# Turning the normalised inputs of a transformer block with transposing DMAs instead of TensorE

## The reference

```
x = x + layernorm(attention(layernorm(x)))
x = x + layernorm(ffn(layernorm(x)))

attention:  q, k, v = split(h @ w_qkv.T + b_qkv)         # h is the normalised input
            per chunk, with a state S (32 x 32) per head:
              out = (q * decay_q) @ S + ((q @ k.T) * mask) @ v
              S   = lam_c * S + (k * decay_k).T @ v
            out @ w_out.T + b_out
ffn:        gate = silu((h @ fp8(gate_w)) * gate_scale)  # fp8() rounds to e4m3, I = 1536
            up   = (h @ fp8(up_w)) * up_scale
            ((gate * up) @ fp8(down_w)) * down_scale
```

## Time and profile before

| | |
|---|---|
| median of three runs | 1149.89 us |
| profiled execution: span from first to last instruction | 1146.1 us |
| what lies around the span (1149.89 - 1146.1) | 3.8 us |
| busy: TensorE, DVE, POOL, ACT | 92%, 64%, 55%, 34% |
| one steady slot | 62.9 us |
| stack copies: number, size, time to landing | 480, 64 KB, 2.1 us |

### The profile page before, as it was taken

How to read it: one execution, slowest core, us unless ns; L and a number is a source line. 1 busy time by engine, 2 the same in 40 slices (tenths; PEclk the granted TensorE clock), 3 DMA queues, 4 the chain that set the end, 5 groups by cost and what they waited for, 6 DMA issues and landing times.

```text
span 1146.1 us, 23001 instructions
## 1 busy us (share of the span) xinstructions
PE 1053.1 (92%) x8772; PEld 795.6 (69%) x8772; DVE 738.0 (64%) x1415; ACT 391.7 (34%) x752; POOL 630.1 (55%) x659
## 2 busy tenths in 40 slices
PE   2646869999999999999999999999999999999887
PEld 1435549595968778595968677695959687786654
DVE  7869996574747475665747474666657475756542
ACT  3222435242433425152424334252424233342211
POOL 0557656474646565465647465555656464656433
PEclk9855979999999999999999999999999999999989
DMA  9211420403022120304031221204040312212000
GB/s 360 83 55 55 100 49 1 102 10 85 28 56 57 38 75 20 86 10 102 10 72 40 53 59 34 71 18 95 11 102 11 68 44 49 63 30 55 10 19 19
DMA packets 83629, 66.10 MB, mean 58 GB/s; under 512 B 9281, under 2 KB 70849, under 8 KB 83393
## 3 DMA queue, kind: packets, MB, share of 16 engines
q1 hardware_dynamic: 82656, 64.00, 21.6%
q10 hardware_dynamic: 864, 0.61, 0.2%
HBM read 24.72 MB, written 8.39 MB: 29 GB/s over the span
## 4 chain that ended last, share of the span: by engine, by line
PE 77%; DVE 13%; POOL 4%; issue 4%; DMA 1%; ACT 0%; POOLq 0%; DVEq 0%; SPq 0%
PE bank L513 29%; PE bank L621 13%; PE bank L528 11%; PE bank L603 6%; PE bank L635 5%; PE bank L565 3%; PE bank L569 2%; PE bank L552 2%; DVE stats L994 2%; PE bank L583 2%; POOL rstd L712 1%; PE bank L441 1%; DVE ffn_pool L932 1%; PE bank L595 1%; DVE up_q L939 1%
## 5 line engine op out<-in xcount | busy, mean ns | idle before, releaser
L788 POOL TENSOR_TENSOR att_pool<-p,att_pool 128x512 f16<-128x512 f32 x128 | 149.8, 1191 | 78.1 <-ACT att_pool L371 78.1
L513 PE MATMUL bank<-ffn_pool,gate_q 128*128 128x256 f16 x1536 | 185.1, 274 | 3.8 <-DVE ffn_pool L1209 3.8
L621 PE MATMUL bank<-x_hl,wqkv_hi 128*128 128x256 f16 x1024 | 172.2, 275 | 13.9 <-DVE wqkv_lo L923 13.9
L513 PE MATMUL bank<-ffn_pool,up_q 128*128 128x256 f16 x1536 | 184.2, 273 | 0.0
L528 PE MATMUL bank<-down_q,ffn_pool 128*128 128x512 f16 x768 | 170.7, 379 | 1.0 <-DVE ffn_pool L1099 1.0
L513 PEld LDWEIGHTS bank<-ffn_pool,gate_q 128*128 128x128 f16 x1536 | 148.9, 98 | 21.4 <-DVE ffn_pool L1209 4.1
L513 PEld LDWEIGHTS bank<-ffn_pool,up_q 128*128 128x128 f16 x1536 | 150.6, 98 | 18.1
L775 POOL TENSOR_TENSOR ffn_pool<-ffn_pool 128x512 f16<-128x512 f32 x96 | 111.2, 1158 | 94.4 <-ACT ffn_pool L385 92.9
L371 ACT CAST att_pool<-p 128x512 f16<-128x512 f32 x128 | 77.9, 618 | 190.7 <-DVE p L1089 190.7
L1099 DVE SCALAR_TENSOR_TENSOR ffn_pool<-bank,us_t,ffn_pool 128x256 f32<-128x256 f32 x192 | 84.1, 479 | 89.9 <-PE bank L513 87.7
L621 PE MATMUL bank<-x_hl,wqkv_lo 128*128 128x256 f16 x512 | 141.0, 275 | 0.0
(11 more groups left out here) (123 smaller groups left out, 1715.1 us busy)
## 6 DMA issues: line engine op xcount, KB each, us to landing
att_pool<-att_pool SPq DMA_DIRECT2D x480, 64.0 KB, 2.1
x_t<-in_x SPq DMA_DIRECT2D x16, 512.0 KB, 3.8
out_x<-ffn_pool SPq DMA_DIRECT2D x32, 256.0 KB, 2.1
att_pool<-in_w_qkv_t SPq DMA_DIRECT2D x4, 768.0 KB, 8.0
ffn_pool<-in_gate_w SPq DMA_DIRECT2D x4, 768.0 KB, 12.8
ffn_pool<-in_up_w SPq DMA_DIRECT2D x4, 768.0 KB, 4.2
ffn_pool<-in_down_w SPq DMA_DIRECT2D x4, 768.0 KB, 4.7
mask<-in_mask_c SPq DMA_DIRECT2D x1, 1024.0 KB, 16.9
```

The costliest lines, as they stand in the source:

```text
L513: ins = nc.tensor.matmul(b[:, j * TOK:(j + 1) * TOK], w[:, k, o * P:(o + 1) * P], x1_hl[:, part, k], start=(k == 0 and part == 0), stop=(k ...
L621: ins = nc.tensor.matmul(b_t[i % 2][:, j * TOK:(j + 1) * TOK], (wqkv_hi, wqkv_lo)[a][:, k, o * P:(o + 1) * P], x_hl[:, b, k], start=(k == ...
L788: nc.gpsimd.tensor_tensor(pr_hl[:, 1, heads(s, g)], by_head(p32[:, g % 2]), pr_hl[:, 0, heads(s, g)], ALU.subtract).then_inc(p_lo_d, 1)
```

## The change

The fp32 values in `nrm` are no longer turned by TensorE. ACT casts them to the hi half and DVE subtracts to the lo half while they are still tokens x channels, into a new tensor `nrm_hl` in SBUF; then SP turns both halves of a tile with one transposing DMA (128 partitions x 1024 fp16, 256 KB, as eight blocks of 128x128) straight into `x_hl` or `x1_hl`. There are four such DMAs in a slot, 64 in all. x1 is split at the end of slot s, behind each `x1_normalise`, and no longer at the start of slot s + 1. The waits of TensorE go to the new semaphores `x_turned` and `x1_turned`.

```diff
+        nrm_hl = sb("nrm_hl", [P, T, 2, D], F16)
@@ SP, start
                 for k in range(KT):
                     sp.dma_start(w_stage[:, k], w_qkv_t[k * P:(k + 1) * P, :]).then_inc(w_in[k], 16)
+                for t in range(T):
+                    turn_x(0, t)
                 for n in range(3):
                     sp.dma_start(stage_for(n), piece_in(n)).then_inc(f_in[n], 16)
...
                 for n in range(3, 12):
                     sp.wait_ge(f_q_d, n - 2)
                     sp.dma_start(stage_for(n), piece_in(n)).then_inc(f_in[n % 3], 16)
+                    if n == 8:
+                        for t in range(T):
+                            turn_x(1, t)
                 stack(1)
+                for t in range(T):
+                    turn_x1(0, t)
+
+            def turned(half, t):
+                return half[:, :, :, t * P:(t + 1) * P].rearrange("p s k c -> p (s k) c")
+
+            def turn_x(n, t):
+                sp.wait_ge(x_lo_d, 2 * n + t + 1)
+                sp.sem_inc(turn_seen, 1)
+                sp.dma_start_transpose(turned(x_hl, t), nrm_hl[:, t].rearrange("p s d -> p (s d)")
+                                       ).then_inc(x_turned, 16)
@@ SP, slot (turn_x1 is turn_x with x1_lo_d, x1_hl and x1_turned)
                 if nxt:
+                    for t in range(T):
+                        turn_x(s + 1, t)
                     stack(s + 1)
+                if att:
+                    turn_x1(s, 0)
+                if att and not nxt:
+                    turn_x1(s, 1)
                 store(s - 1, 0)
+                if att and nxt:
+                    turn_x1(s, 1)
@@ ACT
             def split_x(n):
-                for j in range(2):
-                    act.wait_ge(x_tr, 2 * n + j + 1)
-                    nc.scalar.copy(x_hl[:, 0, 2 * j:2 * j + 2].rearrange("p k t -> p (k t)"),
-                                   b_s[j][:, :]).then_inc(x_hi_d, 1)
+                if not (type(n) is int and n < 2):
+                    act.wait_ge(x1_turned, 32 * n - 32)
+                elif n == 1:
+                    act.wait_ge(x_turned, 32)
+                for t in range(T):
+                    act.wait_ge(nrm_d[LN_X], 2 * n + t + 1)
+                    nc.scalar.copy(nrm_hl[:, t, 0], nrm[:, t]).then_inc(x_hi_d, 1)
+
+            def split_x1(v, t):
+                act.wait_ge(x_turned, 32 * v + (64 if type(v) is not int or v < last else 32))
+                act.wait_ge(nrm_d[LN_X1], 2 * v + t + 1)
+                nc.scalar.copy(nrm_hl[:, t, 0], nrm[:, t]).then_inc(x1_hi_d, 1)
@@ ACT, end of slot
+                if att:
+                    split_x1(s, 0)
+                if nxt:
                     v_hi(s + 1)
+                if att:
+                    split_x1(s, 1)
@@ PE: transpose_x and the transposes at the slot's start are gone
             def gate_up(v, i):
                 if i == 0:
-                    pe.wait_ge(x1_lo_d, 2 * v + 2)
+                    if type(v) is int and v == 0:
+                        pe.wait_ge(norms_d, 3)
+                    else:
+                        pe.wait_ge(y2_d, 2 * v)
+                    pe.wait_ge(x1_turned, 32 * v + 32)
...
             def project_qk(n, i):
-                pe.wait_ge(x_lo_d, 2 * n + 2)
+                pe.wait_ge(x_turned, 32 * n + 32)
@@ DVE (x_lo likewise; the two subtractions from PSUM at the slot's start are gone)
+            def x1_lo(v, t):
+                dve.wait_ge(x1_hi_d, 2 * v + t + 1)
+                nc.vector.tensor_tensor(nrm_hl[:, t, 1], nrm[:, t], nrm_hl[:, t, 0], ALU.subtract
+                                        ).then_inc(x1_lo_d, 1)
@@ DVE, end of slot
                     x1_moments(s, m, 1)
                     v_sum(s + 1, 1)
                     x1_normalise(s, m, 1)
+                    x1_lo(s, 1)
                 y2_scale(v, 1)
```

More of the change, by code:

```diff
@@ L393, in slot @@
                 v = s - 1
-                for j in range(2):
-                    act.wait_ge(x1_tr, 2 * v + j + 1)
-                    nc.scalar.copy(x1_hl[:, 0, 2 * j:2 * j + 2].rearrange("p k t -> p (k t)"),
-                                   (b_y, b_att)[j][:, :]).then_inc(x1_hi_d, 1)
                 if att:
@@ L434, in _ @@
         def _(pe):
-            def transpose_x(n):
-                pe.wait_ge(nrm_d[LN_X], 2 * n + 2)
-                for j in range(2):
-                    for kk in range(2):
-                        for t in range(T):
-                            ins = nc.tensor.transpose(b_s[j][:, kk * TOK + t * P:kk * TOK + (t + 1) * P],
-                                                      nrm[:, t, (2 * j + kk) * P:(2 * j + kk + 1) * P], eye[:, :])
-                    ins.then_inc(x_tr, 1)
             def start():
                 pe.wait_ge(eye_in, 16)
-                transpose_x(0)
                 for i in range(4):
@@ L649, in slot @@
                 v = s - 1
-                pe.wait_ge(nrm_d[LN_X1], 2 * v + 2)
-                for j in range(2):
-                    for kk in range(2):
-                        for t in range(T):
-                            ins = nc.tensor.transpose((b_y, b_att)[j][:, kk * TOK + t * P:kk * TOK + (t + 1) * P],
-                                                      nrm[:, t, (2 * j + kk) * P:(2 * j + kk + 1) * P], eye[:, :])
-                    ins.then_inc(x1_tr, 1)
                 if att:
@@ L1013, in x_lo @@
             def x_lo(n):
-                for j in range(2):
-                    dve.wait_ge(x_hi_d, 2 * n + j + 1)
-                    nc.vector.tensor_tensor(x_hl[:, 1, 2 * j:2 * j + 2].rearrange("p k t -> p (k t)"), b_s[j][:, :],
-                                            x_hl[:, 0, 2 * j:2 * j + 2].rearrange("p k t -> p (k t)"),
-                                            ALU.subtract).then_inc(x_lo_d, 1)
+                for t in range(T):
+                    dve.wait_ge(x_hi_d, 2 * n + t + 1)
+                    nc.vector.tensor_tensor(nrm_hl[:, t, 1], nrm[:, t], nrm_hl[:, t, 0], ALU.subtract
+                                            ).then_inc(x_lo_d, 1)
+            def x1_lo(v, t):
+                dve.wait_ge(x1_hi_d, 2 * v + t + 1)
+                nc.vector.tensor_tensor(nrm_hl[:, t, 1], nrm[:, t], nrm_hl[:, t, 0], ALU.subtract
+                                        ).then_inc(x1_lo_d, 1)
             def start():
@@ L1078, in start @@
                 x1_normalise(0, 0, 1)
+                x1_lo(0, 0)
+                x1_lo(0, 1)
                 scale_h()
@@ L1206, in slot @@
                 v = s - 1
-                for j in range(2):
-                    dve.wait_ge(x1_hi_d, 2 * v + j + 1)
-                    nc.vector.tensor_tensor(x1_hl[:, 1, 2 * j:2 * j + 2].rearrange("p k t -> p (k t)"),
-                                            (b_y, b_att)[j][:, :],
-                                            x1_hl[:, 0, 2 * j:2 * j + 2].rearrange("p k t -> p (k t)"),
-                                            ALU.subtract).then_inc(x1_lo_d, 1)
                 if att:
@@ L1262, in slot @@
                         x1_normalise(s, m, t)
+                        x1_lo(s, t)
                 elif att:
@@ L1267, in slot @@
                     x1_normalise(s, m, 0)
+                    x1_lo(s, 0)
                 y2_scale(v, 0)
@@ L1336 @@
     laid.update({name: a.astype(np.float32) for name, a in constants().items()})
-    nc = bacc.Bacc("TRN2", target_bir_lowering=False, num_devices=1)
+    nc = bacc.Bacc("TRN2", target_bir_lowering=False, num_devices=1, dynamic_dma_scratch_size=4096)
     arrays, args = {}, {}
```

31 lines of the change are left out of this document (16 added, 15 removed).

## The result

The changed kernel takes 1265.26 us (median of four, 1263.11 to 1268.87), against 1149.69 us before: 1.1012 of the time before, 95% interval 1.0993 to 1.1031. Forecast were 1300 us and a range of 1190 to 1420. The profiled execution spans 1261.2 us against 1146.1, so 115.1 us are to be explained.

What follows compares the result with a forecast made beforehand. TensorE's order was taken to set the time in slots 1 to 15. Fourteen slots of 2.6 + 2.6 + 4.9 us (141.4), start 8.3 and end 0.4, added to 1149.9, gave 1300 us, range 1190 to 1420.

Steps and rivals of the forecast that it cites:

- What can be gained is 28 us, and TensorE's order sets the time: Slots 1 to 15: nothing waits on TensorE; removing 2 x 8 transposes a slot can gain 28 us over 16 units.
- `kd` has no slack; +2.6 us ahead of the carry: Slot's end: x1's split lengthens DVE's tail, `kd` comes late, TensorE idles 3.5 us; +2.6 us a slot, transpose saving included.
- x1's DMA is hidden by the late carry: Slot's end: x1's second half lands at 547.1, before gate would start at 547.4, so it adds no wait.
- The transposing DMA: D = 2.0, landing 3.5: SP or DMA engines are free for the next transposing DMA after D = 2.0 us; data land 1.5 us later.
- the low end (0.35) nor the high end (5.2): Bounds for D in us: issue of a 256 KB store, or eight blocks each going like a 64 KB stack copy.
- The pause ahead of the projection: +2.6: Slot's middle: TensorE idles 3.45 us for x's DMAs and projects at 574.1 instead of 571.52; +2.6 us a slot.
- DVE's two subtractions for x keep their lengths: Slot's middle: x's split stays in place, with subtractions from 567.93 ending at 568.6 and 569.2.
- Rival 4: Not slower: TensorE regains 28 us, 1122 us; also DVE operations on SBUF inputs stretch beside POOL, 11 us more. Chance 0.03.
- The clock: 2 x 2.45 = 4.9 us a slot: Behind both new pauses TensorE drops to half clock, losing 2.45 us each, taken from one 3.84 us idle.
- Rival 2: Both pauses: D near 2, but pauses of 3.5 us keep the clock, giving 1231 us. Chance 0.13.
- The start: 8.3: First units: turning DMAs delay loads behind them on SP, 3.3 and 3.2 us, and x1 splits add 1.8; together 8.3.
- The end: 0.4: End of slot 15: x1's second half lands at about 1104.4 against gate's start at 1104.01, costing 0.4 us.

Runs made afterwards that it cites:

- lo_late: Changed kernel with DVE's two x1 subtractions moved, the first behind `y2_moments`, the second behind `k_decay`: 1268.69 us.
- halves: Changed kernel with each transposing DMA of 256 KB split into two of 128 KB, hi issued right behind ACT's cast: 1289.56 us.
- x_early: Changed kernel with the split of x moved forward, ACT's casts behind `h_hi(v, 2)`, DVE's subtractions behind `o_max(s, 0)`: 1237.36 us.
- the two candidates: Changed kernel with x alone turned by DMA, first loads ahead, x split earlier, silu(4) ahead of `probs_hi`: 1151.8 us; with DVE's two x subtractions apart: 1163.28 us.
- filler: Changed kernel with eight matmuls that nobody reads added on TensorE in the pause ahead of the carry: 1246.18 us.
- loads_first: Changed kernel with unit 0's turning DMAs behind all first loads and unit 1's behind piece 9: 1254.53 us.

## Why the prediction came out right, step by step

- *What can be gained is 28 us, and TensorE's order sets the time.* Right; the transposes left, and each place where they stood turned into a wait.
- *`kd` has no slack; +2.6 us ahead of the carry.* Right: a pause of 3.60 where 3.5 was forecast, ended by `k_decay`. The mean is +2.59; a plain slot has +2.9, and the pauses of slots 6 and 10 before, which "nothing waits there" overlooked, bring it down. x1's split cost DVE 1.4 to 1.5 us a half. lo_late took the subtractions out and the pause shrank to 1 us.
- *x1's DMA is hidden by the late carry.* Right: no wait for it ahead of gate(0) in the slots after; lo_late brought it out, 2.2 us.
- *The transposing DMA: D = 2.0, landing 3.5.* Near in sum, for partly other reasons, which is luck. SP is free after 1.25 us and the data land after 3.1. The issue does not go by bytes, as halves showed, while I had reasoned so. Neither the low end (0.35) nor the high end (5.2) holds. The Trainium skill (Advanced Engine Details and Errata, X-Bar Transpose (TRN2)) calls transposing DMAs as fast as regular ones. Here 256 KB take 3.1 us to land against 2.1 for a store of 256 KB and 1.25 us of SP against 0.35, so a single small one is not. The Trainium skill (VectorE: DVE Perf Modes, The three transpose paths) has 1309 ns for one block; eight in one DMA landed in 3.1 us, so that figure does not multiply.
- *The pause ahead of the projection: +2.6.* Gate(0) to projection lost 2.4 us (2.42, and 22.34 instead of 22.39 in the slots that keep the clock): a pause of 2.27 us in the mean (2.07 to 3.01), ended by the DMA, and 0.65 for silu(4), less the 0.88 of the transposes. (A wait costs some 0.16 us more than its idle time, since groups of matmuls overlap by that where none waits.) The way there was another: the second DMA left when the second subtraction was done, 559.05, and not when SP was free of the first, and it landed at 562.3, 0.8 us sooner than 2 x 2.0 + 1.5 behind the first's issue (557.57) gives. That the sum came within 0.2 us is luck. The missed step is silu(4): I named the work that the transposes leave, and did not ask what they had covered. It took the place of a part of the other pause, so it cost nothing extra; in x_early and the two candidates it, or `product(v, 4)` behind it, became the limit.
- *DVE's two subtractions for x keep their lengths.* Wrong: 2.25 instead of 1.28 us in 11 of 14 slots, with both inputs in SBUF and POOL at work. Rival 4 had named that for x1_lo, where it came to 0.1 us.
- *The clock: 2 x 2.45 = 4.9 us a slot.* This is the mis-sized term. By the table, clock cost 1.32 + 0.19 (gate(0) to gate(5): 22.53 against 22.34 where the clock is kept) = 1.5 behind the carry's pause and 0.52 behind the projection's, 2.0 in all. The first pause loses the clock nearly always, but mostly gives it back sooner than the one row I had: 1.4 to 1.7 us in eight of 15 slots, 2.5 to 2.9 in five, nothing in two. The second, of 2.1 instead of 3.45 us, lost it in 4 of 14 slots, with pauses of 2.27, 3.01, 2.62 and 2.47. 14 x (4.9 - 2.0) = 41 us too much, more than the distance between 1300 and 1265, and the start's missing 4.9 us and the ends hide a part of it. filler shows that the term is real: 19 us for matmuls in one pause. Rival 2 (pauses of 3.5 us keep the clock) falls with the granted 0.57 behind the carry's pause.
- *The start: 8.3.* It was 13.2. The order of steps was right (`magic(0)` 6.6 us late, piece 9's rounding 11.7), but DVE's subtractions of x(1) took 5.06 us for two, beside POOL, where each had taken 0.69 before, and the turn behind them waited as long. loads_first took back 10.7.
- *The end: 0.4.* It was about 1.2; TensorE's wait there is 5.77 us instead of 3.84.

The sum was 150.1 and the span grew by 115.1: slots 100.7 instead of 141.4, start 13.2 instead of 8.3, end 1.2 instead of 0.4. The sign, the two pauses and the lost clock held; the size of the clock's term was taken from a single row of a longer pause.

## What to carry to other kernels

Before work is taken off the engine that sets the time, list what waits behind it: here eight transposes of 0.88 us were the cover of silu(4) and `product(v, 4)`, and eight more stood ahead of `kd`; taking them away gave waits there. A pause of TensorE costs its length and often 1.4 to 2.9 us of clock behind it in this kernel, so an edit that only shortens a pause from one place and lengthens it at another may gain nothing. Move a transpose to the DMA queues only where some 3.1 us from the last input to the first use, and the conversion ahead of them, are covered.
